# Softmax pieces one slot apart in a two-layer graph kernel, with TensorE's carry products a slot ahead

## The reference

```python
x = layernorm(x + L0(x, edge_attr, src, dst, ...))       # messages, mean over the edges of a node
h = x
for l in range(2):                                        # relational attention, 8 edge types
    xw = einsum('nf,rfg->rng', h, W[l])
    out_j, out_i = xw[edge_type, src], xw[edge_type, dst]
    logits = leaky_relu((out_i @ q[l] + out_j @ k[l])[:, 0], 0.2)
    alpha = segment_softmax(logits, dst, n)
    h = relu(segment_sum(alpha[:, None] * out_j, dst) + b[l])
out = layernorm(x + h)
```

## The kernel before

| | part 0 starts | part 0 ends | sums of groups 0 to 7 | part 1 starts | part 1 ends | sums of groups 8 to 13 |
|---|---|---|---|---|---|---|
| before | 38 | 52 | 57, 61, ... 85 | 66 | 80 | 89, 93, ... 109 |

## Time and profile before

### The profile page before, as it was taken

One profiled execution on the slowest core, in us unless ns is written; L12 is line 12 of the kernel. 1 busy time (PEld: TensorE's weight loads), 2 busy tenths in 40 slices (PEclk: granted clock), 3 DMA queues, 4 the chain that ended last, 5 costly groups with the idle time before them and its releaser, 6 DMA issues.

```text
span 952.8 us, 10537 instructions
## 1 busy us (share of the span) xinstructions
PE 670.1 (70%) x3022; PEld 435.3 (46%) x3022; DVE 749.6 (79%) x1445; ACT 615.3 (65%) x1425; POOL 583.9 (61%) x506
## 2 busy tenths in 40 slices
PE   2745665666555499999898788559999998777200
PEld 2524444555443355555465455436555654334100
DVE  3478977888778688988999998577979889999920
ACT  1569997889879866655677767566666553434620
POOL 4777777777771388887710000088888756667874
PEclk9559777677777589999999889569999999989655
DMA  8276656657554422323455366323231241142110
GB/s 226 84 215 199 202 172 207 201 160 207 179 165 136 154 73 97 101 70 131 155 167 160 95 199 193 98 93 103 68 130 52 77 169 45 44 146 70 44 44 29
DMA packets 87764, 122.96 MB, mean 129 GB/s; under 512 B 14188, under 2 KB 66854, under 8 KB 87707
## 3 DMA queue, kind: packets, MB, share of 16 engines
q1 hardware_dynamic: 69483, 99.36, 33.0%
q0 software_dynamic: 15680, 21.55, 8.1%
q10 hardware_dynamic: 2544, 1.38, 0.6%
HBM read 87.79 MB, written 45.05 MB: 139 GB/s over the span
## 4 chain that ended last, share of the span: by engine, by line
DVE 27%; PE 23%; POOL 19%; ACT 12%; issue 12%; DMA 5%; SPq 1%; POOLq 0%; DVEq 0%; ACTq 0%
PE ps_y L727 13%; POOL xs L471 11%; DVE work L1320 6%; ACT stage L808 5%; POOL xd L471 5%; DVE ys L1145 5%; DVE st L1073 4%; POOL out L540 2%; DVE opT L1320 2%; DVE ys L1292 2%; PE ps_k L717 2%; ACT xd L824 2%; PE ps_t L689 2%; PE ps_t L588 1%; DVE xd L1298 1%
## 5 line engine op out<-in xcount | busy, mean ns | idle before, releaser
L808 ACT ACTIVATE stage<-stage,nm,rs 128x128 f32<-128x128 f32 x800 | 319.7, 484 | 20.0 <-DVE nm L1069 20.0
L727 PE MATMUL ps_y<-work,wr 128*128 128x512 f32 (+1 forms) x528 | 228.9, 564 | 30.7 <-DVE work L1320 30.5
L471 POOL DMA_INDIRECT xs<-h_table,posI x98 | 130.3, 1330 | 168.0 <-DMA h_table<-ys 138.4
L471 POOL DMA_INDIRECT xs<-x_table,posI x98 | 127.5, 1301 | 62.1 <-DMA x_table<-xd 32.5
L1073 DVE BATCH_NORM_STATS2 st<-stage 128x6 f32<-128x256 f32 x400 | 144.6, 418 | 23.0 <-DMA stage<-in_x 21.9
L1320 DVE SCALAR_TENSOR_TENSOR work<-typB,xs 128x896 f32<-128x896 uint8 x132 | 142.5, 1087 | 18.1 <-ACT xs L773 9.2
L727 PEld LDWEIGHTS ps_y<-work,wr 128*128 128x128 f32 x528 | 97.6, 196 | 127.7 <-issue 69.5
L540 POOL DMA_INDIRECT out<-xd,outI x98 | 110.3, 1126 | 54.2 <-issue 28.3
L471 POOL DMA_INDIRECT xs<-in_x,srcI x98 | 103.6, 1057 | 43.5 <-issue 28.7
L471 POOL DMA_INDIRECT xd<-in_x,dstG x98 | 110.2, 1125 | 30.2 <-issue 29.0
L727 PE MATMUL ps_y<-opT,wr 128*128 128x512 f32 (+1 forms) x256 | 112.2, 562 | 14.5 <-DVE opT L1320 14.5
(11 more groups left out here) (208 smaller groups left out, 1043.1 us busy)
## 6 DMA issues: line engine op xcount, KB each, us to landing
stage<-in_x SPq DMA_DIRECT2D x39, 640.0 KB, 4.1
out<-stage SPq DMA_DIRECT2D x39, 640.0 KB, 3.1
xs<-alpha_rows SPq DMA_DIRECT2D x28, 448.0 KB, 5.5
x_table<-xd SPq DMA_DIRECT2D x14, 448.0 KB, 3.0
h_table<-ys SPq DMA_DIRECT2D x14, 448.0 KB, 3.4
work<-in_src SPq DMA_DIRECT2D x13, 448.0 KB, 5.1
ys<-in_edge_attr SPq DMA_DIRECT2D x6, 896.0 KB, 8.9
sameB<-same_rows SPq DMA_DIRECT2D x42, 112.0 KB, 3.4
```

The costliest lines, as they stand in the source:

```text
L471: nc.gpsimd.indirect_dma_start(out=buf[:, t, :], out_offset=None, in_=table, in_offset=bass.IndirectOffsetOnAxis(ap=idx[:, t:t + 1], axis= ...
L727: mm = pe.matmul(ps_y[:, u, lo:hi], wr[:, r, :], rows, start=(r == 0), stop=(r == R - 1))
L808: ins = a.activation(slot(c)[:, r, :], slot(c)[:, r, :], ACT.Identity, bias=nm[:, h, n:n + 1], scale=rs[:, h, n:n + 1])
```

## The change

Three things move; no arithmetic is added or taken away, and POOL's list of instructions is the same.

1. Pieces of a part stand in consecutive slots instead of every second. Part 0 now ends in slot 45 and part 1 in slot 73, so every sum stands seven slots earlier: 50, 54, ... 78 and 82, 86, ... 102. ACT's exponential follows its piece (slot N0 + 4 instead of N0 + 8), and SP's stores and spreads of the weights move along.
2. TensorE's carry product for piece p stands at the end of slot N0 + p - 1, a slot ahead of the DVE piece that feeds it.
3. In layer 1 the last dense step runs in the third slot of its group (51) instead of the seventh (55), on DVE and ACT.

```diff
-    STORE = [n + 2 * (PIECES - 1) for n in N0]
+    STORE = [n + PIECES - 1 for n in N0]
     SUMS = [STORE[0] + 5 + 4 * g for g in range(HA)]
...
-                        if n in range(N0[half], STORE[half], 2):
-                            carry((n - N0[half]) // 2)
+                        if N0[half] <= n + 1 < STORE[half]:
+                            carry(n + 1 - N0[half])
...
-                        if n == N0[half] + 8:
+                        if n == N0[half] + 4:
                             act.wait_ge(s_arg[j], half + 1)
...
-                    if j == 1 and r == R - 1 and k == K_E[j]:
+                    if j == 1 and r == 3 and k == K_E[j]:
                         bulk_step(BC + 1, first=False)
...
-                        if n in range(N0[half], STORE[half] + 1, 2):
-                            chain((n - N0[half]) // 2, half)
+                        if N0[half] <= n <= STORE[half]:
+                            chain(n - N0[half], half)
...
-                    if j == 1 and n < END and r == R - 1 and K_M[j] + g == K_E[j]:
+                    if j == 1 and n < END and r == 3 and K_M[j] + g == K_E[j]:
                         bulk_step(BC + 1, first=False)
```

## The result

Over 20 runs of each the changed kernel takes 948.34 us at the median (943.05 to 958.01), the kernel before 952.91 (948.79 to 955.42): a difference of 4.6 us. One execution of the changed kernel (958.01) was in the slow state and is left out of the ratio, which is taken from the fast executions: 0.9957, 95% interval 0.9942 to 0.9972. That is a gain of 0.4%, small but clear of the noise. The profiled execution of after took 952.45 us, 4.1 above its own median, that of before 954.62, 1.7 above its one. So the two traces lie 2.2 us apart, and their stages have to be compared one by one, not their ends.

The account below looks back on a forecast made before the run. From the softmax on, the order of DVE's work was taken to bound the kernel, POOL's pace its end. Layer 0 -3.7 and layer 1 -2.8 made -6.5 us: 946.3, with 1.8 around it 948.1, median 947.1; range 938 to 957.

Parts of the forecast that it names:

- Pace of part 0: Slots 38 on: eight slots with close pieces take 28.6 us, 3.6 each, with TensorE starved about 1 us a slot.
- The rival of the thin cover: Both parts: pieces wait for TensorE's work two slots before; 0.27 us at 24 waits eats the 6.5; about 953 us, chance 0.24.
- Rounds at layer 0's end: Behind layer 0's last product: two rounds of relu, turning back and copying instead of four, 12.9 us instead of 23.0, -10.1.
- Exponentials: DVE's waits for ACT: part 1 1.1 us in layer 0 and 1.8 in layer 1, new; part 0 1.6, -0.3 each.
- First sums: First sum of each layer waits for its spread weights: between none and 2 us, taken as 0.7 us each.
- POOL from group 8 on: Layer 1's end: scatters from group 8 to the last take 60.1 us instead of 58.5, +1.6.
- Layer 0 up to its last product: Two more sums +6.6 us, slack at last masks -1.7, exponentials +1.1 and -0.3, first sum +0.7.
- Layer 1 up to group 8: Group 8's sum moves from slot 89 to 82: -7.0 us, then +1.8 - 0.3 + 1.2 - 0.8 + 0.7: -4.4.
- The roots: Layer 1, DVE's waits for ACT's root: last dense step 3.2 us, +1.2; the other six a fifth less, -0.8.
- the signs that I had named: Trace checks: group 8's first scatter some 8 us earlier, last scatter some 6.5; wrong if the clock falls in the parts.
- put seven masks: Both layers: moving each sum seven slots puts seven masks, 1.0 us each, behind it; DVE's work to layer end unchanged.
- The clock rival: Both parts: starved TensorE products run at half clock, 21 us lost against 6.5 gained; about 968 us, chance 0.12.

## Why the prediction was right, and which of its terms were not

Predicted 947.1 us with a range of 938 to 957, measured 948.34. The steps of the forecast that held:

- **Pace of part 0:** 28.6 us forecast for eight slots, 28.1 and 28.2 measured. TensorE's thin cover was enough: carries were waited for 0.67 and 0.38 us in layer 0's part 1 and nowhere else. The rival of the thin cover falls. The slot ahead has a part in that: without it the carries of layer 0's part 1 are waited for 2.6 us and the kernel takes 1.004 of before.
- **Rounds at layer 0's end:** forecast 12.9 us instead of 23.0 (-10.1), measured 12.1 (-10.9).
- **Exponentials:** forecast 1.6 in part 0 and 1.1 and 1.8 in part 1; measured 1.3, and 1.2 and 1.8.
- **First sums:** no wait for their weights; I had allowed 0.7 us each.
- **POOL from group 8 on:** forecast 60.1 us, measured 57.4, under the 58.5 of before. The two intervals at DVE's pace came as forecast (10.5 each); it is the next that I had at 12.2 us and that took 9.8. So this term was mis-sized too, in the change's favour: -1.1 us where I had +1.6.

Two stretches came out longer than their terms, and one omission is in both:

- **Layer 0 up to its last product:** the terms ahead of the rounds add up to +6.4 us; the mask of slot 38 standing in the same place, the last product ends 10.7 us later. The 6.6 us for two more sums were there; the waits were not as forecast. DVE's waits from slot 38 to 97 add up to 8.2 us in before (three for the last masks, 1.7 together, and 1.9 for the exponential among them) and 12.4 in after, 4.3 more where my terms gave -0.2. The key copy (2.2), a root (1.6), carries (1.1) and two products in slots 49 and 50 (2.0) are new; the slack at the last masks gave back 0.8 and not 1.7. The product waits are at least in part this one execution's: the run with part 1 a slot later, the same kernel up to slot 66, waited 0.5 us there. With the rounds that makes -0.2 us for the layer instead of -3.7.
- **Layer 1 up to group 8:** -4.4 forecast; group 8's sum stands 1.0 us earlier, of which 0.3 is layer 0's shift, so -0.7. The roots are not the reason: their waits rose by 0.5 us (3.5 to 4.0 between slots 38 and 97), where I had +1.2 - 0.8. The key copy (2.9), which the forecast did not have, and waits for products in slots 50 and 66 (1.5 and 0.7; 0.2 in before) fill the gap.

So of the signs that I had named, group 8's first scatter came 1.1 us earlier and not 8, and the last scatter 2.2 us earlier and not 6.5. The step that failed is the one on which both stretches rest: that the seven slots by which each sum moves only "put seven masks" behind it instead of ahead. I followed each sum's own parts, and the piece's waits, but not the sum's back rows and last norms into the slots of the last key scores. The experiments show the cause of the key wait from three sides: with the sums at their old place it is absent, with the key scores ahead of the back rows on TensorE it falls from 2.24 to 0.46 us in layer 0 (but only to 2.1 in layer 1), and with part 1 a slot later it is gone. The kernel gains some 6 us by the second and some 8 by the third; about 3 of these 8 are the exponential's waits of part 1, which go as well.

The clock rival (968 us) was not right, but not empty. TensorE's clock fell twice in part 1 of each layer, which I had named as a sign that I was wrong: behind 3.96 and 3.97 us of waiting for piece 1, and behind 3.15 and 4.16 us of waiting for the piece behind the exponential. It also fell at the end of part 0 in layer 1. In part 0 it was 1.00 up to 452.4 in layer 0 and up to 742.5 in layer 1, and from slot 38 to 97 the mean granted clock is 0.96 in layer 0 (0.95 in before) and 0.93 in layer 1 (0.98), far from the half clock that the rival needs. By the Trainium skill ("TensorE: Matmul & The Clock Gate", section "Why this matters for your kernels") long idle gaps between bursts put the clock back; the rows agree in kind, 2.18 and 2.25 us of idle time left it whole, 3.00 and 3.96 did not. But the length of one gap doesn't decide it: behind 2.15 us at 452.52 the clock was 0.50, with another gap of 2.07 us (446.16) a few products ahead. What the falls cost is not measured by itself. In layer 0's part 1 DVE waited 0.67 and 0.38 us for the carries around the slow product; in the run with TensorE's key scores first, where the clock stayed whole there, it did not wait for them.

That the predicted time came out 1.2 us from the measured one owes something to chance. Two misses of opposite sign stand in it: the waits that I did not foresee (4.3 us in layer 0, 3.7 in layer 1) against the end of POOL's work (2.7 us) and 0.8 us in layer 0's rounds. That leaves a gain of 2.0 us of the 6.5 in the traces. By them layer 1 begins 0.3 us earlier and its last scatter ends another 1.9 earlier, together half of the 4.6 us between the medians. The rest is within what single executions differ by: where both kernels are the same, after's profiled execution was 2.1 us faster up to layer 0's slot 0 and 2.0 us slower from there to slot 38. Which stage holds that rest can't be said from one profile each. Nor is it settled why the close pieces with late sums lose all of 17 us: the traces name some 10 us more of waits for roots and products in layer 1, while 3.6 us in layer 0 was a load of `stage` that I can't put down to the edit.

## What to carry to other kernels

When work is moved in a table of slots, follow not only what its instructions wait for but with what else they now share a slot, on every engine that has a part of it: here the moved sums' back rows landed ahead of a producer that everything waited for, and that cost about as much as the change gained. Where a consumer waits on such a producer, one slot more for it, or the producer ahead of its neighbours on its own engine, is cheap to try, and gave more (some 6 and 8 us) than the change itself (4.6). But a copy moved to the front of an in-order queue holds up everything behind it as long as its input is late: the same reorder gained 6 us on TensorE and lost 16 us on ACT.

## What was not expected of the hardware

Switching ACT between the exponential and the root cost a table load of 1.28 us each time (nine such loads in after), and the next activation starts 0.02 us behind it. The Trainium skill ("ScalarE: Activation LUTs", section "What ACT_TABLE_LOAD costs") counts a drain of about 1.38 us on top; no row here shows one: from 790.09 to 791.39 above the load is all there is, and the measurement decides. Which root pays for the load matters: in slot 45 it was hidden, in slot 51 it stood inside a wait of DVE.
